# Attention with two residual layers: the last two units in query halves, two chunks of the last batch projected among the last tiles

## The reference

```python
q, k, v = (proj(Wq), proj(Wk), proj(Wv))            # x @ W.T, 16 heads of 32
scores = einsum('bhsd,bhtd->bhst', q, k) * scale
scores = where(mask, -inf, scores)
attn = softmax(scores, axis=-1)
out = einsum('bhst,bhtd->bhsd', attn, v) -> (B, S, E)
out = out @ Wo.T
xn = out / sqrt(mean(out * out) + EPS) * rms_scale
x = x + xn * (1.0 + sc) + shift                      # sc, shift from the conditioning
x = x + hamilton(q_left_n, hamilton(filtered x, q_right_conj))
```

## Time and profile before

| | |
|---|---|
| median of three runs | 899.29 us (898.95 to 899.41) |
| profiled execution, its time | 899.34 us |
| its span, first to last instruction | 897.6 us |
| mean granted TensorE clock | 0.987 |
| PE busy | 851.8 us (95%) |
| DVE busy | 641.2 us (71%) |
| ACT busy | 613.0 us (68%) |
| POOL busy | 487.9 us (54%) |

### The profile page before, as it was taken

The page is one execution under the profiler, slowest core; times in us unless marked ns, Lnnn a source line. Parts: engine busy times, 40 slices in busy tenths (PEclk is TensorE's granted clock), DMA queues, the critical chain, the costliest instruction groups (busy, mean ns, idle before and its releaser), DMA issues.

```text
span 897.6 us, 16964 instructions
## 1 busy us (share of the span) xinstructions
PE 851.8 (95%) x5254; PEld 633.6 (71%) x5254; DVE 641.2 (71%) x1514; ACT 613.0 (68%) x1491; POOL 487.9 (54%) x348
## 2 busy tenths in 40 slices
PE   6999999999998999999999999999999999999970
PEld 5788888888886566767776777667776777677740
DVE  4611321322328788999999899989999999989868
ACT  5322222322228998999899989999999999998820
POOL 0999980000000111566776577757775677667774
PEclk9999999999999999999999999999999999999995
DMA  8844554653797746785787577785777578755201
GB/s 276 337 164 177 222 181 172 229 189 141 245 292 202 176 96 146 169 204 118 171 203 163 147 181 157 156 207 124 163 181 198 118 172 207 161 143 119 71 24 47
DMA packets 82305, 153.74 MB, mean 171 GB/s; under 512 B 8472, under 2 KB 9112, under 8 KB 82224
## 3 DMA queue, kind: packets, MB, share of 16 engines
q1 hardware_dynamic: 82224, 152.75, 62.8%
HBM read 102.35 MB, written 50.36 MB: 170 GB/s over the span
## 4 chain that ended last, share of the span: by engine, by line
PE 88%; DVE 6%; issue 3%; ACT 1%; DMA 0%; DVEq 0%; SPq 0%; POOL 0%; ACTq 0%
PE banks L654 23%; PE banks L682 13%; PE banks L86 12%; PE banks L365 10%; PE banks L366 10%; PE banks L367 10%; PE banks L698 9%; DVE probs L94 2%; PE banks L663 2%; DVE turned_probs L734 1%; DVE probs L565 1%; ACT probs L103 1%; DMA raw<-in_xT 0%; DVE probs L792 0%; DVE v_sb L804 0%
## 5 line engine op out<-in xcount | busy, mean ns | idle before, releaser
L103 ACT ACTIVATE probs<-probs,least 128x512 f32<-128x512 f32 x512 | 363.6, 714 | 0.0
L94 DVE CUSTOM_DVE_ANT_0 probs<-banks,mask_bias 128x512 f32<-128x512 f32 x512 | 331.5, 680 | 35.3 <-PE banks L86 35.3
L654 PE MATMUL banks<-ident,probs 128*128 128x128 f32 x2048 | 309.2, 273 | 9.9 <-DVE turned_probs L734 3.0
L654 PEld LDWEIGHTS banks<-ident,probs 128*128 128x128 f32 x2048 | 246.3, 141 | 85.5 <-issue 29.1
L86 PE MATMUL banks<-k_rows,q_rows 128*128 128x512 f32 x512 | 245.1, 481 | 0.0
L734 DVE COPY turned_probs<-banks 128x512 f32<-128x512 f32 x256 | 175.8, 687 | 17.0 <-PE banks L654 17.0
L835 ACT ACTIVATE turned_probs<-banks 128x512 f32<-128x512 f32 x256 | 151.1, 590 | 52.7 <-PE banks L654 52.1
L304 DVE SCALAR_TENSOR_TENSOR late<-banks,late 128x512 fp32r<-128x512 f32 x64 | 43.9, 689 | 172.8 <-ACT late L270 172.8
L565 POOL TENSOR_TENSOR late<-rot,late 128x2048 f32<-128x2048 f32 x27 | 124.2, 4600 | 0.0
L270 ACT ACTIVATE late<-banks 128x512 fp32r<-128x512 f32 x64 | 38.3, 598 | 119.1 <-PE banks L367 119.1
L682 PE MATMUL banks<-turned_probs,v_sb 128*32 128x512 f32 x1024 | 116.5, 595 | 0.7 <-ACT turned_probs L835 0.7
(11 more groups left out here) (106 smaller groups left out, 1258.2 us busy)
## 6 DMA issues: line engine op xcount, KB each, us to landing
q_rows<-q_scratch SPq DMA_DIRECT2D x128, 256.0 KB, 6.1
k_rows<-k_scratch SPq DMA_DIRECT2D x128, 256.0 KB, 6.9
q_scratch<-late SPq DMA_DIRECT2D x64, 256.0 KB, 2.3
k_scratch<-late SPq DMA_DIRECT2D x64, 256.0 KB, 2.3
v_scratch<-v_out SPq DMA_DIRECT2D x32, 256.0 KB, 2.1
v_sb<-v_scratch SPq DMA_DIRECT2D x8, 1024.0 KB, 11.9
raw<-in_xT SPq DMA_DIRECT2D x7, 1024.0 KB, 5.6
late<-in_x SPq DMA_DIRECT2D x28, 256.0 KB, 6.2
```

The source lines that it names most:

```text
L94: dve.tensor_tensor_reduce(self.probs[:, n % RING, :], self.ps[:, n % 4, :], self.mask_bias[:, n % TC, :], 1.0, 3e38, ALU.add, ALU.min, se ...
L103: act.activation(self.probs[:, n % RING, :], self.probs[:, n % RING, :], ACT.Exp, bias=self.least[:, u % 2, n % TILES:n % TILES + 1], scal ...
L654: last = pe.transpose(turn_ps[:, place(n) % 2, j * P:(j + 1) * P], probs[:, n % RING, j * P:(j + 1) * P], ident[:, :])
```

## The change

The units are now taken in *groups* v: units 0 to 29 whole, then units 30 and 31 for the chunks 0 and 1 (v 30 and 31), then both for the chunks 2 and 3 (v 32 and 33), eight tiles each. Each group has its own values (half as wide), inverse, scale, norm and split. Chunks 26 and 27 are projected two matmuls a tile in v 30 and 31; chunks 28 and 29, the first two of the last batch, in v 32 and 33; only 30 and 31 follow the last tile. GpSimd rotates chunks 0 to 28, VectorE 29 to 31. From group 29 on ScalarE makes the high part and VectorE the low part of the split; from group 30 on VectorE writes the inverse directly in the spread form (256 elements). The last batch's x is loaded at v 30.

```diff
+ALL, HALVES = tuple(range(TC)), ((0, 1), (2, 3))
+GROUPS = [(u, ALL) for u in range(U - 2)] + [(u, half) for half in HALVES for u in (U - 2, U - 1)]
+V = len(GROUPS)
+ORDER = [(v, u, i, c) for v, (u, chunks) in enumerate(GROUPS) for i in range(HG) for c in chunks]
...
+NORM_AT, INVERT_AT, HI_AT, LO_AT = 3, 0, 4, 5
+MASKS = {16: (0, 2, 2, 1, 1, 1, 1, 1, 2, 0, 2, 0, 1, 0, 1, 1), 8: (0, 2, 2, 1, 1, 1, 0, 1)}
+EXPS = {16: (0, 7, 0, 1, 1, 0, 1, 1, 0, 2, 0, 2, 0, 0, 1, 0), 8: (0, 3, 0, 1, 1, 1, 1, 1)}
+CHUNKS, TAIL = TC * B - 2, (TC * B - 2, TC * B - 1)
+POOL_CHUNKS, POOL_SPLITS, POOL_SPREADS, LATE_X = CHUNKS - 1, V - 5, V - 4, TC * (B - 1)
+PROJECT = {(m + NG, 2 + part): [(m, part)] for m in range(V - 4 - NG) for part in range(12)}
+for m in (V - 4 - NG, V - 3 - NG):
+    PROJECT.update({(m + NG, 2 + part // 2): [(m, part), (m, part + 1)] for part in range(0, 12, 2)})
+PROJECT.update({(V - 2, 2 + part // 2): [(CHUNKS - 2, part), (CHUNKS - 2, part + 1)] for part in range(0, 8, 2)})
+PROJECT.update({(V - 2, 6): [(CHUNKS - 2, 8)], (V - 1, 0): [(CHUNKS - 2, part) for part in range(9, 12)]})
+PROJECT.update({(V - 1, 2 + part // 3): [(CHUNKS - 1, part + j) for j in range(3)] for part in range(0, 12, 3)})
+SQUARE = {(m + NG + 1, 0): m for m in range(CHUNKS - 2)} | {(V - 1, 2): CHUNKS - 2, (V - 1, 7): CHUNKS - 1}
+RESCALE = {(m + NG + 1, 1): m for m in range(CHUNKS - 2)} | {(V - 1, 2): CHUNKS - 2, (V - 1, 7): CHUNKS - 1}
+RESIDUAL = {(m + NG + 1, 2): m for m in range(CHUNKS - 2)} | {(V - 1, 4): CHUNKS - 2}
...
+                if v == V - 4:
+                    sp.wait_ge(valued, NG * (B - 1))
+                    for c in range(TC):
+                        sp.dma_start(v_sb[:, 0, c, :], x[B - 1, c * P:(c + 1) * P, :]).then_inc(tail_in[c], 16)
...
-                        last = pe.matmul(value_ps[i * D:(i + 1) * D, :], v_sb[:, b % 2, j, h * D:(h + 1) * D],
-                                         turned_probs[:, (HG * u + i) % SLOTS, j, :], start=(j == 0), stop=(j == TC - 1))
...
+                        last = pe.matmul(value_ps[i * D:(i + 1) * D, cols], v_sb[:, b % 2, j, h * D:(h + 1) * D],
+                                         turned_probs[:, (HG * u + i) % SLOTS, j, cols], start=(j == 0), stop=(j == TC - 1))
+                last.then_inc(valued, 1)
...
+            values(V - 1)
+            turn_scale(V - 1)
             for parts in (range(9), range(9, 12)):
-                for c in range(TC):
+                for m in TAIL:
...
+                else:
+                    dve.wait_ge(scale_turned, v)
+                    dve.reciprocal(inv_d[:, chunks], den[:, v % 2, :, chunks].rearrange("p i c -> p c i").unsqueeze(3)
+                                   .to_broadcast([P, len(GROUPS[v][1]), HG, D])).then_inc(spread, 1)
...
+            def split_lo(v):
+                u, chunks = GROUPS[v]
+                b, g, cols = u // NG, u % NG, span(chunks)
+                dve.wait_ge(o_hi_ready, v + 1)
+                dve.tensor_tensor(o_lo[:, b % 2, g, cols], o_T[:, cols], f32(o_hi[:, b % 2, g, cols]),
+                                  ALU.subtract).then_inc(o_ready, 1)
...
+                if t == NORM_AT and v > 0:
+                    norm(v - 1)
+                if t == LO_AT and v > POOL_SPLITS:
+                    split_lo(v - 1)
+                if not by_act(n - 1) and n > 0:
+                    move_out(n - 1)
+            invert(V - 1)
+            residual(CHUNKS - 1)
+            norm(V - 1)
+            split_lo(V - 1)
+            dve.wait_ge(turned, N)
             dve.wait_ge(stored[1], 16 * (CHUNKS // 2 - 1))
...
+            rotate(CHUNKS - 1, acc[:, 1])
+            for j, m in enumerate(TAIL):
+                tail_rescale(j, m)
+                tail_residual(j, m)
+                rotate(m, tail_out[:, j])
...
+            def split_hi(v):
+                u, chunks = GROUPS[v]
+                b, g, cols = u // NG, u % NG, span(chunks)
+                act.wait_ge(normed, v + 1)
+                act.activation(o_hi[:, b % 2, g, cols], o_T[:, cols], ACT.Copy).then_inc(o_hi_ready, 1)
...
-                rotation_products(pool, mix, x_s[:, c % 2]).then_inc(mixing, 1)
+                rotation_products(pool, mix, x_of(m)).then_inc(mixing, 1)
+                if m == POOL_CHUNKS - 1:
+                    tail_rms(0)
...
+            for v in range(V):
+                if 0 < v <= POOL_SPREADS:
+                    spread_inverse(v - 1)
+                if v > NG and v - NG - 1 < POOL_CHUNKS:
+                    rms(v - NG - 1)
+                if 0 < v <= POOL_SPLITS:
+                    split(v - 1)
+                if v > NG and v - NG - 1 < POOL_CHUNKS:
+                    rotate(v - NG - 1)
+                if NG <= v < V - 2:
+                    shift(v - NG)
+                if v >= V - 2:
+                    for m in range(LATE_X + 2 * (v - V + 2), LATE_X + 2 * (v - V + 3)):
+                        shift(m)
+            for j in (1, 2):
+                tail_rms(j)
```

More of the change, by code:

```diff
@@ L532, in attention @@
         rotated = sem("rotated")
[L534 to L542, removed]
+        PLACES = []
+        for n, (v, u, i, c) in enumerate(ORDER):
+            if n == FIRST[v] + SCALE_AT and v > 0:
+                PLACES.append(("scale", v - 1))
+            PLACES.append(("tile", n))
+        PLACES.append(("scale", V - 1))
+        PLACE = {what: at for at, what in enumerate(PLACES)}
         def by_act(n):
@@ L548, in place_free, with span @@
         def place_free(eng, at):
[L550 to L557, removed]
+            kind, n = PLACES[at] if at >= 0 else (None, 0)
+            if kind == "scale":
+                eng.wait_ge(scale_out, n + 1)
+            elif kind == "tile" and by_act(n):
+                eng.wait_ge(out_act, n // 2 + 1)
+            elif kind == "tile":
+                eng.wait_ge(out_dve, n // 2 + 1)
+        def span(chunks):
+            return slice(chunks[0] * P, (chunks[-1] + 1) * P)
         def take_waits(eng):
@@ L615, in _ @@
             sp.wait_ge(mod_stored, 16)
-            for u in range(U):
+            for v, (u, chunks) in enumerate(GROUPS):
                 b, g = u // NG, u % NG
[L618 to L621, removed]
+                if NG <= v < NG + LATE_X:
+                    load_x(v // NG - 1, v % NG)
+                if v >= NG + 2:
+                    store(v - NG - 2)
                 if u + 2 < U:
@@ L656, in turn, with turn_scale @@
                 last.then_inc(turned, 1)
[L658 to L663, removed]
+            def turn_scale(v):
+                pe.wait_ge(spread, v + 1)
+                at = PLACE["scale", v]
+                place_free(pe, at - 2)
+                for c in GROUPS[v][1]:
+                    last = pe.transpose(turn_ps[:, at % 2, c * P:(c + 1) * P],
@@ L697, in project @@
                 right = wo_lo if way == 1 else wo_hi
-                last = pe.matmul(y, left[:, b % 2, k, t], right[:, k, :], start=(part == 0), stop=(part == 11))
+                last = pe.matmul(y_of(m), left[:, b % 2, k, t], right[:, k, :], start=(part == 0), stop=(part == 11))
                 if part == 11:
                     last.then_inc(y_ready, 1)
[L702 to L707, removed]
+            for n, (v, u, i, c) in enumerate(ORDER):
+                t = n - FIRST[v]
+                if t == VALUES_AT and v > 0:
+                    values(v - 1)
+                if t == SCALE_AT and v > 0:
+                    turn_scale(v - 1)
@@ L708, in _ @@
                 if n + SCORE_AHEAD < N:
                     scores.score(pe, n + SCORE_AHEAD)
[L710 to L711 removed]
+                for m, part in PROJECT.get((v, t), ()):
+                    project(m, part)
                 turn(n)
[L713 to L715 removed]
+            values(V - 1)
+            turn_scale(V - 1)
@@ new lines, in _ @@
+            for c in range(TC):
+                dve.wait_ge(v_stored[c], 16 * B)
+            masks = MASK_AHEAD
+            for n, (v, u, i, c) in enumerate(ORDER):
+                t = n - FIRST[v]
+                if t == INVERT_AT and v > 0:
+                    invert(v - 1)
+                for _ in range(MASKS[FIRST[v + 1] - FIRST[v]][t]):
+                    if EARLY_END <= masks < N:
+                        scores.mask(dve, masks)
+                    masks += 1
+                if (v, t) in RESCALE:
+                    rescale(RESCALE[v, t])
+                if (v, t) in RESIDUAL:
+                    residual(RESIDUAL[v, t])
+                if t == NORM_AT and v > 0:
[4 more added lines that the diff above has]
+                    move_out(n - 1)
```

342 lines of the change are left out of this document (142 added, 200 removed).

## The result

The changed kernel takes 901.40 us (median of 7 runs, 899.40 to 902.48), the kernel before 899.14 us in runs beside it: a ratio of 1.0025, 95% interval 1.0013 to 1.0037. The forecast was 895.6 and a gain; it is a small loss. The profiled execution is the shortest of the seven: 899.40 us, span 897.6, the span of before. Its unit 30 begins 1.2 us earlier than that of before (VectorE's first rescale there at 818.07 against 819.25), so from there on it is 1.2 us longer than before, at the same span.

A forecast was written before the change was run, and what follows sets the result against it. TensorE bounds the kernel until 869.4, then a VectorE chain; in the last groups VectorE and GpSimd become a relay. Summed in time order, VectorE ends at 891.2, plus 2.7 store: span 893.9 against 897.6, so 895.6 us, range 887 to 900.

The forecast's parts named there:

- PE: TensorE's own work from 818.16 on, priced at 49.6 us: it could end at 867.8 instead of 869.4.
- The relay: Last groups: GpSimd's rotations and VectorE's residuals take turns, each beginning when the other ends; GpSimd 10.5 us each half group.
- rival A: Last groups: VectorE's low split meets no running GpSimd product, so no holds or lateness; 887 us, chance 0.17.
- Half-width values in 1.9 us: TensorE in the half groups: values at half width take 1.9 us, between bounds of 1.8 and 3.6.
- Holds of the low split: VectorE in v 31 and 32: the low split waits 1.9 us for GpSimd's product, the copy out queued behind it.
- The residual of 29 held by GpSimd's addition: Tail: GpSimd's 2.39 us addition starts first, so VectorE's residual 29 comes at 870.4 to 871.1.
- PE idle of 1.8 us ahead of a turned tile: v 31 and 32: TensorE, with two turn buffers, waits about 1.8 us for VectorE's held copy out.
- The wide reciprocal: VectorE's half-group inverse on 256 elements instead of 16: 1.42 us, bounds 0.42 and 1.74.
- rival C: VectorE's inverse price per element doubles, 2.6 us for a half group, three ahead of residuals; 898 us, chance 0.10.
- About even: Moving low splits to VectorE costs it two holds of 1.9 us and saves GpSimd 2.0 us a group.
- Rival B: Low split meets the product at its start in v 31 to 33, held 4.6 us; slower, 901 us, chance 0.10.
- D: Half-width values cost nearly the whole price, 1.7 us more in each of four groups; about 899 us, chance 0.08.

The follow-up runs named there:

- rows early: Changed kernel with unit 31's q and k rows loaded in two halves, heads 0 and 1 eight tiles sooner: 894.69 us, ratio 0.9950 to the kernel before; once more 894.44 us.
- late rows: Kernel before, with only the rows of unit 31 loaded 11 scores later: 909.17 us, ratio 1.010 to the kernel before.
- narrow inverse: Changed kernel with unit 31's rows loaded earlier, plus the half groups' inverse taken on 8 elements by VectorE and spread by ScalarE: 890.57 us, ratio 0.9906 to before.

## Why the prediction was wrong

The step that failed is a wait put at nothing. The sum says "PE in v 30 has its first turn at 818.2, values and scale to 823.0", as if unit 31's scores, which are made ahead among these tiles, always found their rows. Measured: TensorE idle for 4.17 us until those rows landed, the first turn of v 30 at 821.29 and values and scale done at 827.38, the values alone 1.0 us slower by the clock; with the rows early the same steps come at 817.07 and 821.6. That one wait, with the clock behind it, is worth 6.7 us in the medians (5.9 in the profiles), more than the whole 5.8 between forecast and result. Under *PE* the forecast moved scores, turns and projections and priced each; under *ACT* and SP it followed only the DMAs that the diff moves. It did not ask of the loads that stay where they are when their data are first wanted in the new order. The kernel's own numbers would have told: the last transfers of a unit's rows start at 813.5 in the trace of before for a first issue at 809.4, each lands after a median of 6.1 to 6.9 us, so the last at about 820, 11 us after the first issue; and 8 tiles without values last 7.3 (at 0.91 us each, scores from 808.59 to 814.94 in the trace of after). Nor was there a rival for it, so the range (887 to 900) left it out.

The relay itself stands. With the rows in time the forecast's kernel takes 894.7 and 894.4 where 895.6 was said. Its steps, start times in us:

| step | forecast | after | rows early |
|---|---|---|---|
| residual 25 | 821.7 | 824.01 | 820.58 |
| residual 26 | 835.0 | 839.67 | 834.11 |
| residual 27 | 847.6 | 852.65 | 847.08 |
| residual 28 | 861.4 | 866.45 | 860.87 |
| DVE's rotation of 29 | 872.8 | 877.11 | 871.52 |
| end of DVE | 891.2 | 894.81 | 889.22 |

The forecast's times count from a unit 30 that begins as in the trace of before; the kernel with rows early began 1.1 us sooner in its profile (residual 25 at 820.58 against 821.7). Against its own start it lost 0.6 us up to the residual of 28 and won 1.4 behind it, of which 0.7 lie ahead of DVE's rotation of 29 and the rest in that rotation and what follows. So the good fit of 895.6 is in part luck of errors that cancel. (Two sums of the record are off by little: 879.8 and 11.3 are 891.1, and rival A's 865.1 with 1.55 and 15.6 is 882.25.)

Point by point, in the trace of after:

```profile
835.75 1.93 PE L701 MATMUL banks<-turned_probs,v_sb 128*32 128x256 f32 x32 [0.16 <-ACT turned_probs L864]
837.62 0.44 PE L682 MATMUL banks<-ident,inv_d 128*128 128x128 f32 x2
```

```profile
873.34 2.42 DVE L795 SCALAR_TENSOR_TENSOR v_sb<-scaled,tail_rstd,v_sb 128x512 f32<-128x512 f32 x1
```

Half-width values in 1.9 us: 1.87 (start to start, 835.75 to 837.62). Holds of the low split of 1.9 us: 1.87, twice. The residual of 29 held by GpSimd's addition: 2.42 us instead of 0.74. PE idle of 1.8 us ahead of a turned tile, put down to the copy out: 1.8. The wide reciprocal is the term that was mis-sized: 1.74 us, 1.66 start to start, against 1.42. That is 6.3 ns an element between 16 and 256, the step from 4 to 8 elements (6.25 ns) and not the one from 8 to 16. It came out at the upper bound of 1.74, not at the doubled price of rival C (2.6 us for the inverse). 6.3 ns is six times the 1.05 ns of a copy's element (0.54 us for 512, by the forecast's split of 0.69 into 0.15 fixed and the rest). The Trainium skill's repeat count of 8 ("VectorE: DVE Perf Modes", section "First, the fixed hardware budget") is not met as eight times that price.

Rival A (a free relay, 887) put 8.6 us on holds and lateness together. Taking the low splits of groups 30 and 31 away gives 3.1 us: the holds are a real price, but under half of A's. "About even" in the paragraph on the page set two holds against 2.0 us a group saved on GpSimd, as if the time of both engines were worth the same; in groups 31 and 32 GpSimd waited for DVE (2.34 us ahead of the product of 27), so DVE's microseconds counted there. The warning in the Trainium skill, "Perfetto Trace Analysis", section "Optimizing Scalar/DVE Operations", that work moved between these two engines may bring nothing, is neither borne out nor refuted: no run here has the low splits of the half groups on GpSimd. Rival B's whole holds (4.6 us) and D's full-price values (3.6 us) are not in the traces, which have 2.29 and 1.87. The median of the result lies where B pointed, 901, but by another mechanism.

## What to carry to other kernels

When a change reorders or halves the work that consumes prefetched data, list every load that it does not touch, with the event that frees its buffer, its volume over the measured rate, and the first use in the new order. Time bought in a tail is lost again if the engine that was bound before stands still ahead of it, and in both kernels that stalled here TensorE's stall cost more than its length. Where two engines hand work to and fro and hold each other up, price the order on the one beside the long instruction of the other, then look for the moment at which the other waits anyway.

## What the runs showed of the hardware

- After 4.2 us without a matmul (815.85 to 820.02) the granted clock stayed at 1.00 until about 820.9, with matmuls running again, and was 0.50 from then to about 824.3; the values took 4.65 us instead of 3.57 to 3.64. In the kernel before with late rows it fell at about 834.8, 5.5 us into its 8.0 us of stall, and was 0.50 until about 841.6. In the kernel with rows early waits of 1.5 to 1.8 us left it at 1.00 (836 to 842, 851 to 853).
- The reciprocal costs 178, 203 (190 in the half groups), 242 and 1744 ns for 4, 8, 16 and 256 elements a partition.
- A two-input VectorE instruction of 0.42 us with both inputs in SBUF waits for the rest of a running GpSimd instruction (0.42 us become 2.29 beside the product). GpSimd's next one can wait in turn: VectorE's residual of 29 runs until 875.76, and the addition L986, started at 875.28, takes 1.63 us instead of 1.28. Where both became ready at the same event, the GpSimd instruction that follows its own power without a wait started first: in the kernel with the narrow inverse the addition at 864.08, VectorE's residual at 864.20, which then takes 2.81 us.
